# The lead-in of a one-core attention and FFN kernel in another order

## The reference

```python
x = x + L0_xattn(layernorm(x), ctx)   # 16 heads of 16; scores/4 - 0.1*|t_q - t_k|, softmax, times V, then Wo and bo
x = x + L0_ffn(layernorm(x))          # product-key retrieval (4 heads, top 8 of 64+64 keys) plus a dense silu FFN
x = x + L1_xattn(layernorm(x), ctx)   # relu(q), relu(k), relu(v), softmax, times V, no output projection
x = x + L1_ffn(x)                     # gate on a layernorm of x, 8 experts, the best 2 by softmax of the gate
```

## Time and profile before

| | before |
|---|---|
| median of 3 runs | 1219.52 us (1215.89 to 1220.21) |
| the profiled execution | 1213.62 us |
| its span, first to last instruction | 1211.8 us |
| mean granted TensorE clock | 0.928 of 2.4 GHz |
| PE busy | 1055.4 us (87%) |
| DVE busy | 788.4 us (65%) |
| ACT busy | 638.7 us (53%) |
| POOL busy | 474.4 us (39%) |

### The profile page before, as it was taken

How to read it: one execution, slowest core, us unless ns; L and a number is a source line. 1 busy time by engine, 2 the same in 40 slices (tenths; PEclk the granted TensorE clock), 3 DMA queues, 4 the chain that set the end, 5 groups by cost and what they waited for, 6 DMA issues and landing times.

```text
span 1211.8 us, 16920 instructions
## 1 busy us (share of the span) xinstructions
PE 1055.4 (87%) x5478; PEld 658.8 (54%) x5478; DVE 788.4 (65%) x1986; ACT 638.7 (53%) x848; POOL 474.4 (39%) x494
## 2 busy tenths in 40 slices
PE   9499899989776999999999778999999888799991
PEld 5134343434355787787777554433334334588881
DVE  3667677786489777877787334777777955244443
ACT  2146565566528667667677422565545661355550
POOL 1347777686413243343443321212323334222220
PEclk9579999999879999999999986999998998899996
DMA  7946778666999300000002330455453328222226
GB/s 186 249 148 192 228 198 264 174 206 224 255 238 233 78 1 1 1 1 1 1 1 64 103 78 1 148 165 146 117 167 93 102 63 325 66 74 71 72 62 209
DMA packets 75595, 151.71 MB, mean 125 GB/s; under 512 B 8234, under 2 KB 45356, under 8 KB 73974
## 3 DMA queue, kind: packets, MB, share of 16 engines
q1 hardware_dynamic: 62518, 99.46, 31.9%
q0 software_dynamic: 10544, 47.23, 11.2%
q10 hardware_dynamic: 2448, 3.94, 1.2%
HBM read 73.88 MB, written 76.25 MB: 124 GB/s over the span
## 4 chain that ended last, share of the span: by engine, by line
PE 55%; DVE 24%; ACT 8%; issue 6%; POOL 3%; DMA 3%; SPq 1%; ACTq 0%; DVEq 0%; POOLq 0%
PE ps L1296 14%; DVE negmax L1589 9%; PE ps L1194 7%; PE ps L1161 6%; PE ps L1140 4%; PE ps L1175 4%; PE ps L1149 4%; PE ps L1398 3%; PE ps L1375 3%; PE ps L1361 2%; PE ps L1203 1%; PE ps L1516 1%; DVE moe_w L1885 1%; DVE hl L1594 1%; DVE on L1609 1%
## 5 line engine op out<-in xcount | busy, mean ns | idle before, releaser
L1589 DVE TENSOR_REDUCE negmax<-ps 128x1 f32<-128x512 f32 x512 | 320.9, 682 | 68.9 <-PE ps L1161 67.2
L905 ACT ACTIVATE pt<-ps 128x1024 f32<-128x1024 f32 x256 | 256.4, 1026 | 129.9 <-PE ps L1175 129.1
L1161 PE MATMUL ps<-sk,sq 56*128 56x512 f32 x512 | 166.5, 460 | 48.0 <-DVE negmax L1589 24.7
L1194 PE MATMUL ps<-pt,v_aug 128*32 128x512 f32 x1024 | 142.6, 620 | 1.2 <-POOL pt L670 0.8
L1161 PEld LDWEIGHTS ps<-sk,sq 56*128 56x128 f32 x512 | 75.7, 200 | 105.3 <-DVE negmax L1589 76.3
L1175 PE MATMUL ps<-sq,sk 57*128 57x512 f32 x512 | 127.1, 489 | 2.5 <-DVE negmax L1589 1.4
L670 POOL TENSOR_TENSOR pt<-pt,near 128x256 f32<-128x256 f32 x128 | 92.3, 728 | 76.0 <-ACT pt L905 75.7
L1175 PEld LDWEIGHTS ps<-sq,sk 57*128 57x128 f32 x512 | 50.1, 190 | 101.2 <-issue 72.4
L835 POOL DMA_INDIRECT expert_out<-yo,dest x39 | 38.2, 980 | 116.2 <-ACT yo L1080 104.5
L751 POOL TENSOR_TENSOR w_first<-w_first,moe_w 128x1024 f32<-128x1024 f32 x16 | 38.1, 2379 | 105.7 <-DVE pt L1877 105.0
L1361 PE MATMUL ps<-sel,hl 128*128 128x512 f32 x256 | 71.7, 412 | 5.6 <-DVE pt L1877 5.6
(11 more groups left out here) (284 smaller groups left out, 2008.2 us busy)
## 6 DMA issues: line engine op xcount, KB each, us to landing
expert_rows<-zero SPq DMA_DIRECT2D x3, 5586.0 KB, 58.0
expert_weights_split<-wst POOLq DMA_DIRECT2D x8, 2048.0 KB, 9.4
qk_rows<-hl SPq DMA_DIRECT2D x30, 512.0 KB
sq<-qk_rows SPq DMA_DIRECT2D x60, 192.0 KB, 4.6
sk<-qk_rows SPq DMA_DIRECT2D x60, 192.0 KB, 5.1
moe_w<-in_w POOLq DMA_DIRECT2D x16, 512.0 KB, 7.1
wexp<-expert_weights_split POOLq DMA_DIRECT2D x16, 512.0 KB, 4.6
wexp<-expert_weights_split SPq DMA_DIRECT2D x4, 2048.0 KB, 17.1
```

Of the source, the lines that this page charges most:

```text
L905: act.activation(pt[:, 4 * (U % 2) + 2 * half:4 * (U % 2) + 2 * half + 2, :], ps[:, 2 + 2 * half:4 + 2 * half, :], ACT.Exp, scale=(BIAS, S ...
L1161: pe.matmul(ps[:, jbank(job), :], sq[r, pair, t * P:(t + 1) * P], sk[r, pair, :], start=True, stop=True).then_inc(s_job, 1)
L1194: ins = pe.matmul(ps[32 * j:32 * j + 32, OBANK, :], v_aug[:, b % 2, c, HG * g + j, :], pt[:, 4 * (U % 2) + j, :], start=(c == 0), stop=(c ...
L1589: dve.tensor_reduce(negmax[:, n % 2, col:col + 1], src, AX, ALU.max, negate=True).then_inc(s_jd, 1)
```

## The change

It reorders the lead-in of the first attention. These are its parts, by engine:

- **SP**: after x and the context of batch 0, the constant rows' source comes first, then `ident` and `st_dist`. The constant rows go out as soon as `rowc` is cast, then the key rows of batch 0, then `w_ret` and `keys`. SP waits for the key rows alone (`s_dk`) and issues all eight key stacks. It waits for group 0 of the stacks, and only then issues x and the context of batch 1, the selector, x of batches 2 and 3 and two tables. The context of batch 2 is issued at step 2 instead of -7.
- **POOL's queue** issues the other six weight and bias loads, behind its memsets.
- **ACT**: the query rows are issued before the v products are emptied, and ACT issues all eight query stacks. It copies the two halves of `wret` twice (as the high part, and whole into spare room), `bo_full` and `gbc`, then takes the roots of batch 1 alone, then the near factor. It casts the selector at step 2.
- **DVE**: casts `rowc` first of all, then the statistics and norm of batch 0, then scales `wq`. Its `prologue()` is gone. The statistics of batch 1 come after step -3, those of batches 2 and 3 after steps 0 and 1, and a seed for their inverse roots after step 2.
- **POOL**: makes `bv_wide` and the scaled gate weights, normalizes batch 1, adds `bo_bc`. In the steps: `add_bo` at 2, 33, 45 and 46, Newton rounds for the roots at 3 and 4, the low part of `wret` at 4 and 8, `norm` of batch 2 at 9 and 14 and of batch 3 at 21 and 26.
- **PE**: the products of `w_ret` and `keys` stay before step -7, with `keep_busy(4)` behind them; those of the gate and of `bv` (`gate_prologue`) come after step -4.
- **Tables**: for the first attention k is prepared before xt, and batches 2 and 3 load their stacks at -11 instead of -12. The second attention keeps its tables.

```diff
-prepared = lambda b: PREPARE_SECOND if b == 1 else PREPARE
-STACKS = (None, 10, 12, 12)
-NEXT_CTX = (-LEAD, -9)
+PREPARE_1 = {-17: ("k", 0), -16: ("k", 1), -15: ("xt", 0), -14: ("xt", 1), -13: ("q", 0), -12: ("q", 1), -11: ("v", 0), -10: ("v", 1)}
+PREPARE_2 = {-21: ("k", 0), -20: ("k", 1), -17: ("xt", 0), -16: ("xt", 1), -15: ("q", 0), -14: ("q", 1), -12: ("v", 0), -11: ("v", 1)}
+PREPARED = ((None, PREPARE_1, PREPARE_2, PREPARE_2), (None, PREPARE_SECOND, PREPARE, PREPARE))
+STACKS = ((None, 10, 11, 11), (None, 10, 12, 12))
+NEXT_CTX = ((2, -9), (-LEAD, -9))
...
+        rows_out = lambda n: 128 * n - 64
...
# SP
             sp.dma_start(x_tok[:, 0], tokens(a["x"][0])).then_inc(s_x[0], 16)
             load_ctx(0, 0)
+            sp.dma_start(st_rows, a["c_rows"]).then_inc(s_rows_in, 16)
+            for dst, src in ((ident[:], a["c_ident"]), (st_dist, a["c_dist"])):
...
+            sp.wait_ge(s_rowc, 1)
+            for dst in (sk, sq):
+                for s in range(2):
+                    const_rows(sp, 0, s, dst)
+            for s in range(2):
+                write_rows(0, 0, "k", s)
+            for dst, src in ((st_wq, a["w_ret"].rearrange("(a n) d -> n a d", n=RD)), (st_keys, a["keys"].rearrange("n h p k -> n (h p k)"))):
+                sp.dma_start(dst, src).then_inc(s_wr, 16)
+            sp.wait_ge(s_dk, 64)
+            for g in range(NG):
+                for s in range(2):
+                    stack(0, 0, g, s, sk)
+            sp.wait_ge(s_ld[0], 64)
+            sp.dma_start(x_tok[:, 1], tokens(a["x"][1])).then_inc(s_x[1], 16)
+            load_ctx(0, 1)
+            sp.dma_start(st_sel, a["c_sel"]).then_inc(s_selin, 16)
+            for b in range(2, B):
+                sp.dma_start(x_tok[:, b], tokens(a["x"][b])).then_inc(s_x[b], 16)
...
# POOL
+            def gate_columns():
+                pool.wait_ge(s_w, 16 * NW)
+                for k in range(KC):
+                    own(pool.tensor_scalar(bv_wide[:, k, :], ones[:], bvc[:, k:k + 1], None, ALU.mult))
+                    own(pool.tensor_scalar(gwb[:, k, :], gw[:, k, 0:ME], gcol[:, KC + k:KC + k + 1], None, ALU.mult))
...
+            def wret_low(k):
+                pool.wait_ge(s_wret, 2 * k + 2)
+                pool.tensor_tensor(wret[:, 1, k, :], wret_full[:, k, :], wret[:, 0, k, :].bitcast(F32), ALU.subtract).then_inc(s_wrl, 1)
...
-            add_bo(0)
+            gate_columns()
             norm(0, 1)
-            add_bo(1)
-            pool.wait_ge(s_selin, 16)
-            pool.tensor_copy(sel[:], st_sel).then_inc(s_sel, 1)
+            bias_out()
...
-                if U in (2, 3):
-                    norm(0, 2, range(2 * U - 4, 2 * U - 2))
-                if U == 4:
-                    add_bo(2)
-                if U in (14, 21):
-                    norm(0, 3, range(0, 2) if U == 14 else range(2, 4))
-                if U == 26:
-                    add_bo(3)
+                if U == 2:
+                    add_bo(0)
+                if U in (3, 4):
+                    rstd_newton(range(0, 2) if U == 3 else range(2, NEWTON))
+                if U in (4, 8):
+                    wret_low((U - 4) // 4)
+                if U in (9, 14):
+                    norm(0, 2, range(0, 2) if U == 9 else range(2, 4))
+                if U in (21, 26):
+                    norm(0, 3, range(0, 2) if U == 21 else range(2, 4))
+                if U == 33:
+                    add_bo(1)
+                if U in (45, 46):
+                    add_bo(U - 43)
...
# ACT
                 for job in table[L]["first"]:
+                    if job.kind == "v" and job.i == 0:
+                        for s in range(2):
+                            first_query_rows(s)
                     empty(L, job)
...
+                    for k in range(KC):
+                        act.wait_ge(s_wret_ps, k + 1)
+                        act.copy(wret[:, 0, k, :], ps[:, 2 + k, :]).then_inc(s_wret, 1)
+                        act.copy(wret_full[:, k, :], ps[:, 2 + k, :]).then_inc(s_wret, 1)
+                    act.wait_ge(s_wret_ps, KC + 1)
+                    act.copy(bo_full, ps[:, OBANK, 0:D]).then_inc(s_wret, 1)
...
+                    sqrt(1, sd[:, 1, :], mv[:, 1, :, 1])
+                    act.wait_ge(s_ci, 16 * NCI)
                     act.activation(near[:], st_dist, ACT.Exp, scale=-BIAS).then_inc(s_nr, 1)
...
# PE
                 if L == 0:
                     prologue()
+                    keep_busy(4)
...
+                    if L == 0 and U == -4:
+                        gate_prologue()
...
# DVE
+                    if L == 0 and U == -3:
+                        batch_stats(1)
+                        dve.sem_inc(s_lnv, 1)
+                    if L == 0 and U == -2:
+                        dve.wait_ge(s_lnd, 2)
+                        dve.reciprocal(rstd[:, 1, :], sd[:, 1, :]).then_inc(s_rstd, 1)
+                    if L == 0 and U in (0, 1):
+                        batch_stats(2 + U)
+                    if L == 0 and U == 2:
+                        flat_bt = lambda v: v.rearrange("p b t -> p (b t)")
+                        root_seed(flat_bt(rstd[:, 2:B, :]), flat_bt(mv[:, 2:B, :, 1]), root[:, 0, 0:2 * TT]).then_inc(s_lns, 1)
...
+            def batch_stats(b):
+                dve.wait_ge(s_x[b], 16)
+                stats(TT * b, x_tok[:, b], range(TT))
+                moments(TT * b, mv[:, b])
...
+            dve.wait_ge(s_rows_in, 16)
+            dve.tensor_copy(rowc[:], st_rows).then_inc(s_rowc, 1)
             dve.wait_ge(s_x[0], 16)
             stats(0, x_tok[:, 0], range(TT))
             moments(0, mv[:, 0])
             dve.sem_inc(s_lnv, 1)
-            dve.wait_ge(s_wqk, 16 * 3)
-            dve.tensor_scalar(wq[0][:], wq[0][:], SCALE * UNITS, None, ALU.mult).then_inc(s_conv, 1)
             dve.wait_ge(s_lnd, 1)
             dve.reciprocal(rstd[:, 0, :], sd[:, 0, :]).then_inc(s_rstd, 1)
             first_norm()
+            dve.wait_ge(s_wqk, 16 * 3)
+            dve.tensor_scalar(wq[0][:], wq[0][:], SCALE * UNITS, None, ALU.mult).then_inc(s_conv, 1)
```

More of the change, by code:

```diff
@@ L521, in attention @@
             def attention(L):
-                if L == 0:
-                    for g in range(NG):
-                        if g == 0:
-                            sp.wait_ge(s_dw, 128)
-                        stack(0, 0, g, 0, sq)
-                        stack(0, 0, g, 0, sk)
-                    sp.wait_ge(s_wret_ps, KC + 1)
-                    sp.dma_start(st_sel, a["c_sel"]).then_inc(s_selin, 16)
                 for U in STEPS[L]:
@@ L1407, in _ @@
             pe.wait_ge(s_sel, 1)
+            pe.wait_ge(s_wrl, KC)
             turn_norm(0)
@@ L1624, in attention @@
                         empty(L, job)
-                if L == 0:
-                    prologue()
                 for U in STEPS[L]:
```

174 lines of the change are left out of this document (85 added, 89 removed).

## The result

The change makes the kernel slower by about one per cent: the median is 1230.25 us (12 runs, 1227.24 to 1233.36) against 1217.57 us for the kernel before on the same chip (12 runs, 1212.94 to 1225.78). The ratio is 1.0105, with a 95% interval of 1.0085 to 1.0126. The forecast was 1215.5 us with a range of 1208 to 1222, so the result lies outside it and has the other sign. The profiled execution took 1230.09 us, with a span of 1228.3 us against 1211.8 before and a mean clock of 0.924 against 0.928.

A forecast was written before the change was run, and what follows sets the result against it. The prediction took TensorE (PE), busy 87% of the span, as the bound, with free time only where PE waits. Its terms summed to -4.0 us, giving 1215.5 us for the median, range 1208 to 1222.

The forecast's parts named there:

- The first score: Start of the first step: fewer bytes ahead of the stacks bring it at 36.5 instead of 47.4 us, -10.9 us.
- PE's wait would be 1 to 3 us: Ahead of the first score: argument for a warm and early start, that PE's wait there would be this short.
- The gate's products: Between steps -4 and -3: products of the gate and of bv now lie on the path, +3.2 us.
- Statistics of batch 1: In a step where DVE is the bound: 1.85 us and 0.2 for the reciprocal, +2.1 us.
- Statistics of batches 2 and 3 with the seed: Steps 0 and 1: 1.85 us on DVE fits beside PE's work except at a step's end, +0.8, bounds 0 and 4.3.
- (c): Rival: stacks of batches 2 and 3 come late, 3.6 us a group; 1229.5 us with four late groups; chance 0.11.
- k before xt: Steps -1 to 2: same four jobs in another order, taken at 0, bounds -2.5 and +1.8 us.
- Norm of batch 2 in step 14: Step 15: the transposes of xt would wait for POOL's norm of step 14, +1.0 us, bounds 0 and 1.8.
- Step 13's wait: Step 13: the 2.06 us wait for a stack stays and shrinks by perhaps -0.2 us.
- (a): Rival, warm and early start: first score at 33, clock 1.00 in steps -7 to 1; about 1208 us; chance 0.20.
- (b): Rival, stacks hardly earlier: constant rows hold key rows until 22, first score at 42 us; 1221 us; chance 0.13.
- nothing gives the gain back later: After the lead-in: the rest of the program follows PE's steps, so the -4.0 us sum is kept.

The follow-up runs named there:

- a2: The changed kernel with the loads of `w_ret` and `keys` issued ahead of the constant rows, filler kept: 1228.38 us, ratio 1.0091.
- a1: The changed kernel without the four filler products `keep_busy(4)` behind PE's prologue: 1227.56 us, ratio 1.0091.
- b1: a2 with the filler replaced by the products of the gate and of bv, which leave step -4: 1222.14 us, ratio 1.0037.
- b2: a2 with x of batches 1 to 3 issued from ACT's queue at the start, all statistics ahead of the first maximum, no seed: 1221.35 us, ratio 1.003.
- d1: b1 with POOL's `add_bo` of batch 0 moved from step 2 to step 10: 1222.5 us in one execution, beside 1220.38 of the kernel before.
- c1: b1 with statistics of batches 2 and 3 in pieces after steps 2 to 5, seed after 7, Newton rounds and batch 2's norm later: 1227.62 us, ratio 1.0086.
- c3: c1 with batch 3's table and stack step of the kernel before, its norm at steps 20 and 21: 1221.5 us, ratio 1.0028.
- c4: c3 with the query stacks' constant rows issued behind the key rows of batch 0: 1220.9 us, ratio 1.0003.
- a3: The changed kernel with the second k product of batch 3 at -18 instead of -20: 1228.19 us, ratio 1.009.
- c2: b1 with the query stacks' constant rows issued behind the key rows of batch 0: 1222.67 us, ratio 1.0025.

## Why the prediction failed

**The first score, -10.9.** It was -2.3 (45.12 against 47.38), outside even the bound of 43. The bytes had the smaller part in it: with `keys` early it came at 38.74 (a2), two microseconds from the predicted 36.5. In after the stacks' group was there by 40.5, four microseconds late, and in a1 by 43.5. The step that failed was to count `w_ret` and `keys` as bytes among others and to leave PE's prologue behind them unpriced. They stood on SP's list behind the constant and the key rows, and PE runs its prologue before it looks at a score. The count had PE's 3.7 us of products and the filler end well ahead of the stacks; in fact the wait for `keys` of 7.31 us dropped the clock, so that the products took 7.09 us, and the filler's 5.88 came on top. "PE's wait would be 1 to 3 us" was true of the stacks only because the same stretch was filled with a worse wait.

**The gate's products, +3.2.** Right: +3.6 (step -4 took 6.00 us against 2.39), and gone in b1.

**Statistics of batch 1, +2.1.** Right: +1.8.

**Statistics of batches 2 and 3 with the seed, +0.8.** Wrong: +4.7 by b2, over the upper bound of 4.3. The step that failed was that 1.85 us of DVE fit beside 4 to 7 us of PE's work. DVE had the room as a sum, but not at a step's end, as the prediction itself noted and then didn't price. PE waited 0.96 and 0.61 us for a bank behind them in after, 1.36 and 0.83 in d1. That is 1.6 to 2.2 of the 4.7 us. The larger part of the rest fits a low clock in steps 0 to 2 (0.50 from 78 to 84 us), for which the bound had no room; b2, without statistics, didn't have it, but c1 had it without them too, so how much of it is theirs stays open. I had priced a clock loss for late stacks, in rival (c), and none here. The seed's 1.9 us beside POOL was no part of the sum either: what it cost in after isn't shown, and at step 7 (c1, c3, c4) it stands at the head of a loss of 9.3 us.

**k before xt, 0.** Right within its bounds: -0.5.

**Norm of batch 2 in step 14, +1.0.** Near: PE waits 0.72 us for it at 141.02. It doesn't show in the lateness, which is the same 7.1 at steps 6 and 26.

**Step 13's wait, -0.2.** It is 1.07 us and no longer 2.06; the mechanism was right, the size -1.0 and not -0.2.

**Batch 3's preparation: no term at all.** +5.2 (steps 26 to 37 in after against before; c3 takes 5.6 us off c1 there, a3 4.5 off after). This is the second largest error. The prediction said of the stacks that "on SP nothing stands between -12 and -11, so they are issued when their buffers come free, as now", and so far it was right: no stack of batch 2 or 3 is waited for. But it read only the move from -12 to -11 and not that batch 3 also changed its table, which puts its second key rows ahead of the maxima's rows in SP's queue. No row of this stretch stood in the prediction.

**The rivals.** (a) had its premise tested by the filler: the full clock does not survive scores at DVE's pace. (b) is not borne out. Its condition wasn't met, for the key rows left at 14.84 and not at 22, and the split of the constant rows lets the key stacks leave 4 us earlier, but in c2 and c4 neither the start nor the median moves by more than they scatter. (c) gave the time (1229.5) for the wrong reason. Its kind of event, a late row in SP's queue and a clock that falls behind it, happened once, with the maxima's rows, and cost 5.2 us and not 3.6.

**The sum as it should have been**, by the runs and against the profiled execution: -2.5 at the first maximum, +3.6, +1.8, -0.5, +4.7 gives +7.1 at step 6, and +5.2 makes +12.3 at step 38, the measured lateness there. The terms are the differences of one execution of each kernel, so that they add up proves nothing; that it is nearly the median's +12.7 is partly luck, since the profiled execution of before lies 4.0 us under its median. The claim that "nothing gives the gain back later" hid that every step up to 38 has its own place where it can.

What stays open: the trace's first maximum of one and the same lead-in lies anywhere from 37.5 to 40.5 us, and no run says why; how much of the low clock in steps 0 to 2 the statistics bring about wasn't separated; and after is behind by 2 to 4 us more in the second attention of its one profile.

## What to carry to other kernels

When loads are reordered, price for each engine the first instruction that waits for a load behind the moved ones, and not only the one that the reordering is meant to serve: two weight loads of 640 KB ahead of an engine's prologue were worth 6 us of start here. Work taken out of an idle lead-in into the steps can cost more than its length: 1.8 us twice and a seed became 4.7 us here, and in c1 a wait of 3.3 us on TensorE was followed by some 14 us at the lower clock. And where a table moves a batch's work by a step, follow what it now stands ahead of in the DMA queue, the smallest and most urgent rows first.

## What was new about the hardware

A vector operation on 128 by 8 numbers took 1.90 to 2.25 us when a POOL operation on 128 by 1024 ran beside it, and 0.16 us without it, while POOL's took 2.35 to 2.37 us either way. Not every operation is stretched so: in c1 four maxima from 95.28 us on took 2.48 us, their usual time, although an operation of the same kind ran on POOL until 96.21. The Trainium skill ("GPSIMD Engine Reference", 1. Specifications) has the two engines share their way to SBUF, and sees contention with vector instructions in a 2-port mode or with two SBUF inputs. The trace agrees that they contend, for an operation with one input in SBUF: it waited out nearly the whole of POOL's. In which mode it ran, the trace doesn't show. The maxima, which weren't stretched, read PSUM.

Moving loads to another issuing engine did not move them out of the way: x from ACT's queue still delayed the key rows by 5.7 us in b2. The same move helped the kernel before, whose x had stood among the last rows and the first stacks.

In after the clock rose to 1.00 behind 5.9 us of dense matmuls (44 to 48 us) and was 0.82 in the next 4 us, with PE busy 3.50 of 4 us at scores that came at DVE's pace.
